# A four-layer graph network in fp32: other column halves and order in its expert layers, additions between weight units, and a new order in its attention

## Chip, cores and metric

One Trainium2 (trn2) chip, one core. The metric is the device time of one execution in microseconds (us), lower is better. TensorE is PE below, VectorE is DVE, ScalarE is ACT, GpSimd is POOL, SyncE is SP.

## What is computed

Four layers, each a graph part and a feed-forward part with residuals, on 625 nodes of 768 features, all in fp32. Cut to what matters here:

```python
x = x + gnn0(layernorm(x))         # g0: softmax aggregation, then 768 -> 1536 -> 768, + bias + input
x = x + moe0(layernorm(x))         # f0: 8 experts, top 2, hidden 192, gelu
x = x + gcn(layernorm(x))          # g1: two graph convolutions
x = x + moe1(layernorm(x))         # f1: 8 experts, top 2, hidden 128, silu, balanced by importance
x = x + gat(layernorm(x))          # g2: attention, 8 heads x 128, relu, then 1 head x 768
x = x + soft_slots(layernorm(x))   # f2
x = x + rgcn3(layernorm(x))        # g3: three relational layers
x = x + moe3(layernorm(x))         # f3: 8 experts, top 2, hidden 192, gelu

# one expert layer (f0, f1, f3)
logits = x @ gate.T;  probs = softmax(logits);  w, i = top_k(probs, 2)
# f1 alone: importance = probs.sum(axis=0); running = 1 + 0.1 * (importance - 1) + 0.01; w = w / running[i]
combine[t, i] = w / sum(w)
y = sum_e combine[:, e] * (act(x @ w1[e]) @ w2[e])

# the attention
e = leaky_relu(a_src[src] + a_dst[dst], 0.2)
alpha = exp(e - max over the node's edges);  out = sum(alpha * h[src]) / sum(alpha)
```

## The kernel before

The 625 nodes are five tiles of 125 (padded to 626 columns where nodes are columns). Every dense fp32 product is three fp32r matmuls on a high and a low part of each operand (`three`, L2501 to L2503: high by high, low by high, high by low). The weights stream in as units of 128 x 768: SP loads each into a ring of three raw slots, POOL splits it into `w_hi` (L867) and `w_lo` (L870), and PE's use of a unit frees its slot (`unit_used`). POOL works through the units in the order in which it is written; other work of POOL stands between them.

All orders are written by hand: each engine's program is a list of steps, and the steps wait on semaphores. `plan_groups` only simulates PE's groups to hand out the eight PSUM banks: a group that opens a bank waits until the bank's last user was read.

**g0.** The MLP's up part has twelve units, its down part twelve more. Between the two, POOL adds the bias to the residual of the five tiles (L881, five additions of 125 x 768), and only then splits unit 12, the down part's first.

**An expert layer** (`expert_layer`, L2640). The normalised rows are transposed tile by tile on PE (`turn_behind`, L2510); ACT copies them as `xT_hi` (L938) and DVE makes `xT_lo` (L1488). The transposes of the last tile are left over and done inside the layer. `router(c)` multiplies the nodes of half c with the gates (L2656, L2658): half 0 is columns 0 to 311 (`CH`), so it waits for the low parts of tiles 0 to 2, half 1 for all. `up(s, j)` is a job: one unit of 128 hidden features against one half of the columns, 18 matmuls. Job j is unit j // 2, half j % 2. `router(1)` stands behind job 0, its transposes for DVE (L2674) behind job 1, f1's sum over all probabilities (L2681) behind job 3. DVE works out the routing (`route`, L1694 to L1744) meanwhile; behind job 5 (`EXPERT_LAG` 6) PE waits for the result `combine`, transposes it (L2688) and, from then on, broadcasts a row of it for each job (L2698), by which DVE weighs the job's activation in one of six slots `tmp`.

```python
router(0)
turn_behind(s)(NT - 1)
for j, spread in enumerate(spread_after(jobs)):
    if j < jobs: up(s, j)
    if j == 0: router(1)
```

**The attention** (g2). PE makes h1 in 20 groups of 125 x 256 (matmuls of 256 columns); ACT copies each out (L1213) and has other steps between the copies. Among these are `powers(h, s)` for the heads h = 0 and 1 and the source tiles s = 0 to 4: two exponentials (L1204, L1205) with which DVE makes `greater_branch` (L2061). Two buffers of them may wait for DVE at most, so the fourth waits for DVE's first. `weights_of_edges` (L2067) is DVE's loop over s; beside it run the ten maxima of scores of later heads (`greatest_score`, L2009). Then, head by head, PE multiplies h1 with the weights (`head_product`, L2919), DVE takes the totals (`head_total`, L2127) and makes the next head's scores (L2086), ACT the means (`head_mean`, L1262) and exponentials. The second part of the attention starts with its own product g2b (five groups for each half), whose banks are fixed numbers 0 to 4.

## Time and profile before

| | |
|---|---|
| median of 3 runs | 1725.19 us (1724.49 to 1728.24) |
| the profiled execution | 1721.06 us, of which the traced span is 1719.3 us |
| PE busy | 1670.1 us (97% of the span), 10227 matmuls |
| DVE, ACT, POOL busy | 53%, 26%, 41% |
| granted clock of PE | nine tenths of full or more in 39 of 40 slices, eight tenths in the second |

Read it so: PE is busy nearly always, so what the profile shows as PE's idle time in front of an instruction, with its releaser, is where time can go or come from. A row of a timeline gives the start, the duration, the engine, line and operation, output <- input, shapes, how many like instructions it joins, and in brackets the idle time before it and what ended that.

### The profile page before, as it was taken

To read this page: it belongs to the slowest core of one execution; us is meant where nothing else is said; L and a number is where in the kernel's file an instruction comes from. 1 tells how busy PE (TensorE), PEld (TensorE's weight loads), DVE (VectorE), ACT (ScalarE), POOL (GpSimd) and SP (SyncE) were. 2 spreads that over 40 slices of the span, in tenths; PEclk is the share of its full clock that TensorE was granted. 3 is DMA by queue.
4 is the path that set the end of the run, shared out by engine and by line. 5 is a ranking of instruction groups with operands and counts; after the bars stand their busy time and mean duration, and the time that the engine had idled before them with its cause. 6 is when DMAs were issued, how large, how long until landed. Compare 5 with 4: busy or idle time off the path is not lost.

```text
span 1719.3 us, 25796 instructions
## 1 busy us (share of the span) xinstructions
PE 1670.1 (97%) x10227; PEld 1571.7 (91%) x10227; DVE 919.6 (53%) x1860; ACT 452.6 (26%) x867; POOL 697.7 (41%) x432
## 2 busy tenths in 40 slices
PE   8799999999999998899999999999999999999999
PEld 7699999997999998899477889899999999998999
DVE  8993537417776688878588453513112141235731
ACT  7443113303223147834132311101001111112310
POOL 1026855661544631350020375442643434342663
PEclk9899999999999999999999999999999999999999
DMA  2002222323212210014010122110211112110222
GB/s 91 1 28 65 76 65 65 132 91 138 65 47 58 78 50 19 12 37 143 19 33 1 31 77 64 54 48 28 83 58 53 58 44 59 52 56 30 65 74 73
DMA packets 41999, 99.83 MB, mean 58 GB/s; under 512 B 10508, under 2 KB 12142, under 8 KB 41894
## 3 DMA queue, kind: packets, MB, share of 16 engines
q1 hardware_dynamic: 37828, 87.87, 16.8%
q10 hardware_dynamic: 4066, 10.46, 1.7%
q8 instruction: 79, 1.29, 0.3%
q14 instruction: 26, 0.21, 0.0%
HBM read 96.39 MB, written 1.92 MB: 57 GB/s over the span
## 4 chain that ended last, share of the span: by engine, by line
PE 84%; DVE 11%; ACT 2%; issue 1%; POOL 1%; POOLq 0%; DVEq 0%; ACTq 0%
PE bank L2501 10%; PE bank L2502 10%; PE bank L2503 10%; PE banks L2501 9%; PE banks L2503 9%; PE banks L2502 9%; PE banks L2995 3%; PE bank L2995 3%; PE banks L3170 2%; PE banks L3175 2%; PE bank L3170 2%; PE bank L3175 2%; PE bank L2919 2%; DVE src_hot L1557 1%; DVE tmp L1893 1%
## 5 line engine op out<-in xcount | busy, mean ns | idle before, releaser
L867 POOL TENSOR_TENSOR w_hi<-raw,ones_r 128x768 fp32r<-128x768 f32 (+1 forms) x192 | 295.8, 1541 | 911.8 <-PE bank L2503 334.1
L870 POOL TENSOR_TENSOR w_lo<-raw,w_hi 128x768 fp32r<-128x768 f32 (+1 forms) x192 | 370.5, 1930 | 15.1
L2501 PE MATMUL bank<-w_hi,xT_hi 128*125 128x384 f32 (+2 forms) x564 | 188.6, 334 | 1.9 <-DVE small L2034 1.5
L2503 PE MATMUL bank<-w_hi,xT_lo 128*125 128x384 f32 (+2 forms) x564 | 187.5, 333 | 0.0
L2502 PE MATMUL bank<-w_lo,xT_hi 128*125 128x384 f32 (+2 forms) x564 | 187.5, 332 | 0.0
L2501 PE MATMUL banks<-w_hi,xT_hi 128*125 128x384 f32 (+2 forms) x436 | 151.0, 346 | 0.0
L2503 PE MATMUL banks<-w_hi,xT_lo 128*125 128x384 f32 (+2 forms) x436 | 150.5, 345 | 0.0
L2502 PE MATMUL banks<-w_lo,xT_hi 128*125 128x384 f32 (+2 forms) x436 | 150.3, 345 | 0.0
L1684 DVE TENSOR_TENSOR hT_lo<-tmp,hT_hi 128x312 fp32r<-128x312 f32 (+1 forms) x88 | 94.2, 1077 | 42.0 <-ACT hT_hi L1012 41.6
L2501 PEld LDWEIGHTS bank<-w_hi,xT_hi 128*125 128x125 f32 x564 | 104.6, 186 | 5.1 <-DVE small L2034 1.7
L2502 PEld LDWEIGHTS bank<-w_lo,xT_hi 128*125 128x125 f32 x564 | 104.6, 186 | 2.3
L2503 PEld LDWEIGHTS bank<-w_hi,xT_lo 128*125 128x125 f32 x564 | 104.5, 185 | 2.4
L2396 DVE TENSOR_TENSOR through_lo<-banks,through_hi 125x384 fp32r<-125x384 f32 (+1 forms) x45 | 25.5, 578 | 138.1 <-ACT through_hi L1417 138.1
L2501 PE MATMUL bank<-w_hi,hT_hi 128*125 128x384 f32 x276 | 93.5, 339 | 1.3 <-ACT mean L1262 0.9
L2503 PE MATMUL bank<-w_hi,hT_lo 128*125 128x384 f32 x276 | 93.2, 338 | 0.0
L2502 PE MATMUL bank<-w_lo,hT_hi 128*125 128x384 f32 x276 | 93.1, 337 | 0.0
L2501 PE MATMUL banks<-xT_hi,w_hi 128*128 128x312 f32 (+1 forms) x282 | 87.5, 310 | 0.1
L2502 PE MATMUL banks<-xT_lo,w_hi 128*128 128x312 f32 (+1 forms) x282 | 86.8, 308 | 0.0
L2503 PE MATMUL banks<-xT_hi,w_lo 128*128 128x312 f32 (+1 forms) x282 | 86.6, 307 | 0.0
L2396 DVE TENSOR_TENSOR through_lo<-bank,through_hi 125x384 fp32r<-125x384 f32 (+1 forms) x45 | 25.7, 582 | 110.6 <-ACT through_hi L1417 110.6
L2501 PE MATMUL banks<-w_hi,hT_hi 128*125 128x384 f32 x244 | 82.7, 339 | 1.6 <-POOL w_lo L870 1.6
L2501 PEld LDWEIGHTS banks<-w_hi,xT_hi 128*125 128x125 f32 x436 | 80.9, 186 | 2.9 <-DVE xT_lo L1635 0.3
(592 smaller groups left out, 3909.7 us busy)
## 6 DMA issues: line engine op xcount, KB each, us to landing
raw<-wa SPq DMA_DIRECT2D x92, 384.0 KB, 3.1
raw<-wc SPq DMA_DIRECT2D x76, 384.0 KB, 3.1
raw<-wb SPq DMA_DIRECT2D x28, 448.0 KB, 3.3
w_rows<-w_in ACTq DMA_DIRECT2D x1, 3072.0 KB, 12.8
bias<-bias_in ACTq DMA_DIRECT2D x6, 384.0 KB
w_first<-w_in ACTq DMA_DIRECT2D x1, 2304.0 KB, 9.7
w_down<-w_down_in SPq DMA_DIRECT2D x8, 288.0 KB, 5.3
w_up<-w_up_in SPq DMA_DIRECT2D x1, 2304.0 KB, 10.8
```

The costliest lines, as they stand in the source:

```text
L867: pool.tensor_tensor(w_hi[:, k, 0:width], raw[:, k, 0:width], ones[:, 0:1].to_broadcast([P, width]), ALU.mult).then_inc(S("unit_high"), 1)
L870: pool.tensor_tensor(w_lo[:, k, 0:width], raw[:, k, 0:width], f(w_hi[:, k, 0:width]), ALU.subtract).then_inc(S("unit_split"), 1)
L1557: TS(src_hot[0:TN, k], iota[:, 0:NODES], source[:, t:t + 1], None, ALU.is_equal).then_inc(S(label + "_hot"), 1)
L1684: TT(hT_lo[:, m, c0:c0 + cn], tmp[:, i % TSLOTS, 0:cn], f(hT_hi[:, m, c0:c0 + cn]), ALU.subtract).then_inc(S(s + "_low"), 1)
L2396: TT(through_lo[c][:, n, 0:width], bank(key + "_through", i)[0:TN, 0:width], f(through_hi[c][:, n, 2 - 2 * c:2 - 2 * c + width]), ALU.subt ...
L2501: tell_used(pe.matmul(dst, l_hi, r_hi, start=start, stop=False))
L2502: pe.matmul(dst, l_hi, r_lo, start=False, stop=False)
L2503: return pe.matmul(dst, l_lo, r_hi, start=False, stop=stop)
L2919: last = pe.matmul(dst[0:TN, at:at + HEAD_DIM + 1], prob_of("g2p", h)[:, s, n * TN:(n + 1) * TN], h1[:, s, h, 0:HEAD_DIM + 1], start=s == ...
L2995: ins = pe.matmul(bank("R", d)[0:TN, c * cn:(c + 1) * cn], source[:, s * TN:(s + 1) * TN], target[:, at], start=t == r_first(p, r) and wid ...
L3170: tell_used(pe.matmul(dst[0:TN, 0:counted + cw], rel[:, r, s, at], through_hi[c][:, s, begin:begin + counted + cw], start=s == 0, stop=False))
L3175: last = pe.matmul(dst[0:TN, counted:counted + cw], rel[:, r, s, at], through_lo[c][:, s, 0:cw], start=False, stop=s == NT - 1)
```

## The change

1. The expert layers split the nodes into columns 0 to 249 and 250 to 625 (`EXPERT_CH`). `router(0)` waits for two tiles. The first four jobs are units 0 and 1 with half 0, then units 0 and 1 with half 1. The left transposes stand behind job 0, `router(1)` behind job 1, its transposes behind job 2, f1's sum behind job 5, and the routing is awaited behind job 6. There are seven slots for activations, each 376 wide.
2. POOL waits for the routing (`combine`) before it splits unit 4 of each expert layer (`held_units`).
3. In g0 POOL does one residual addition and then one unit, five times.
4. In the attention's `weights_of_edges`, two of the maxima go ahead of each `greater_branch`, where they stood behind it; ACT does the head-1 powers of s = 3 and 4 behind the last copy of h1, where they stood between the copies.
5. g2b's groups open banks 4, 5, 0, 1, 2, where they opened 0, 1, 2, 3, 4.

```diff
+EXPERT_CH = [(0, 2 * TN), (2 * TN, NP - 2 * TN)]
-EXPERT_LAG = 6
-IMPORTANCE = 3
+EXPERT_LAG = 7
+IMPORTANCE = 5
+ROUTED_UNIT = 4
+EXPERT_SLOTS = 7
+ROUTER_JOB = 1
+POWERS_BESIDE = 3
+LAST_BANKS = (4, 5, 0, 1, 2)
...
     if s == "g0" and j < 6:
         return j % 3, j // 3
+    if s != "g0" and j < 4:
+        return j % 2, j // 2
     return j // 2, j % 2
...
+        def held_units(engine, first, count, body):
+
+            last = first + count
+            for s in ("f0", "f1", "f3"):
+                hold = FIRST_UNIT["u", s] + ROUTED_UNIT
+                if first < hold < last:
+                    ring_units(engine, first, hold - first, body)
+                    engine.wait_ge(*E(s + "_combine", 4))
+                    first = hold
+            ring_units(engine, first, last - first, body)
...
             for n in range(NT):
                 pool.wait_ge(*E("g0_doubled", n + 1))
                 pool.tensor_tensor(x[0:TN, n], x[0:TN, n], bias[0:TN, 0:D], ALU.add).then_inc(S("g0_residual"), 1)
+                u = UP_UNITS["g0"] + n
+                split(UNIT)(u, u // RING, u % RING)
...
-                if i > NEXT_SHIFT:
+                if NEXT_SHIFT < i <= NEXT_SHIFT + POWERS_BESIDE:
                     powers("g2p", 1, i - NEXT_SHIFT - 1)
...
+            for s in range(POWERS_BESIDE, NT):
+                powers("g2p", 1, s)
             lesser_shifts(2)
...
                 for s in range(NT):
+                    for other, d in beside[2 * s:2 * s + 2]:
+                        if d == 0:
+                            await_group(dve, "g2p_asB", 2 * other + 1)
+                        greatest_score("g2p", other, d)
                     greater_branch("g2p", h, s)
...
-                    for other, d in beside[2 * s:2 * s + 2]:
-                        if d == 0:
-                            await_group(dve, "g2p_asB", 2 * other + 1)
-                        greatest_score("g2p", other, d)
...
-                    pe.wait_ge(*E(s + "_xT_low", (6, 2 * NT)[c]))
+                    pe.wait_ge(*E(s + "_xT_low", (4, 2 * NT)[c]))
...
                 router(0)
-                turn_behind(s)(NT - 1)
...
                     if j == 0:
+                        turn_behind(s)(NT - 1)
+                    if j == ROUTER_JOB:
                         router(1)
-                    if j == 1:
+                    if j == ROUTER_JOB + 1:
                         pe.wait_ge(*E(s + "_routerT_read", 2))
```

The same change as the order of instructions, at three places. POOL in g0, between the last up unit and the down units, before; L881 is the residual addition, L867 and L870 split a unit (high, low):

```order
L870 TENSOR_TENSOR w_lo<-raw,w_hi 128x768
L782 REGISTER_ALU
L782 COMPARE_AND_BRANCH
L881 TENSOR_TENSOR x<-x,bias 125x768 x5
L782 UNCONDITIONAL_BRANCH
L782 ISA
L866 ISA
L867 TENSOR_TENSOR w_hi<-raw,ones_r 128x768
L869 REGISTER_ALU
L870 TENSOR_TENSOR w_lo<-raw,w_hi 128x768
```

and changed (the addition is L918 there, the split L904 and L907):

```order
L918 TENSOR_TENSOR x<-x,bias 125x768
L904 TENSOR_TENSOR w_hi<-raw,ones_r 128x768
L907 TENSOR_TENSOR w_lo<-raw,w_hi 128x768
L918 TENSOR_TENSOR x<-x,bias 125x768
L904 TENSOR_TENSOR w_hi<-raw,ones_r 128x768
L907 TENSOR_TENSOR w_lo<-raw,w_hi 128x768
```

Unit 12 stands behind one addition where it stood behind five.

DVE at the start of the attention's weights of head 0, before; L2009 is a maximum of scores (with the read of its result), L2061 the greater branch of one source tile, L2071 the product with the adjacency:

```order
L2061 SCALAR_TENSOR_TENSOR prob_early_77<-prob_early_77,lesser 125x626
L2009 ISA edge_scores_141,small<-banks,maskT 125x628
L2009 ISA small 125x1
L2009 ISA edge_scores_142,small<-banks,maskT 125x628
L2009 ISA small 125x1
L2061 SCALAR_TENSOR_TENSOR prob_early_77<-prob_early_77,lesser 125x626
L2071 SCALAR_TENSOR_TENSOR prob_early_77<-prob_early_77,adj 125x1252
```

and changed (L2051, L2103 and L2117 are the same three operations):

```order
L2051 ISA edge_scores_148,small<-banks,maskT 125x628
L2051 ISA small 125x1
L2051 ISA edge_scores_149,small<-banks,maskT 125x628
L2051 ISA small 125x1
L2103 SCALAR_TENSOR_TENSOR prob_early_83<-prob_early_83,lesser 125x626
L2051 ISA edge_scores_148,small<-banks,maskT 125x628
L2051 ISA small 125x1
L2051 ISA edge_scores_149,small<-banks,maskT 125x628
L2051 ISA small 125x1
L2103 SCALAR_TENSOR_TENSOR prob_early_83<-prob_early_83,lesser 125x626
L2117 SCALAR_TENSOR_TENSOR prob_early_83<-prob_early_83,adj 125x1252
```

Two more maxima come ahead of the first greater branch; five branches and ten maxima are left in all.

ACT at the end of the copies of h1, before; L1213 is a copy, L1204 and L1205 the two exponentials of one source tile:

```order
L1213 ACTIVATE h_68<-bank 125x2x128 [waits group_closed]
L1204 ACTIVATE prob_early_78<-uB_early_80,small 125x626 [waits greater]
L1205 ACTIVATE lesser<-uB_early_80,small 125x626
L1213 ACTIVATE h_68<-bank 125x2x128 [waits group_closed]
L1204 ACTIVATE prob_early_78<-uB_early_80,small 125x626 [waits greater]
L1205 ACTIVATE lesser<-uB_early_80,small 125x626
L1246 ACTIVATE uB_75<-banks 125x626 [waits group_closed]
```

and changed (the copy is L1253, the exponentials L1244 and L1245):

```order
L1253 ACTIVATE h_68<-bank 125x2x128 [waits group_closed] x2
L1244 ACTIVATE prob_early_84<-uB_early_86,small 125x626 [waits greater]
L1245 ACTIVATE lesser<-uB_early_86,small 125x626
L1244 ACTIVATE prob_early_84<-uB_early_86,small 125x626 [waits greater]
L1245 ACTIVATE lesser<-uB_early_86,small 125x626
L1286 ACTIVATE uB_81<-banks 125x626 [waits group_closed]
```

The last two copies no longer stand behind exponentials that wait for DVE.

## Rows read from the trace of the kernel before

**Rows 1.** The page: span and busy time of the engines.

```profile
span 1719.3 us, 25796 instructions
PE 1670.1 (97%) x10227; PEld 1571.7 (91%) x10227; DVE 919.6 (53%) x1860; ACT 452.6 (26%) x867; POOL 697.7 (41%) x432
```

**Rows 2.** Waits of PE: engine, line, what for; total us, times, longest.

```profile
PE bank L2919 <- ACT mean L1262: 7.3, 7, 1.6
...
PE banks L2656 <- issue: 0.7, 1, 0.7
```

**Rows 3.** Timeline of POOL and PE where g0's up part ends.

```profile
176.76 10.04 POOL L881 TENSOR_TENSOR x<-x,bias 125x768 f32<-125x768 f32 x5
186.76 1.47 POOL L867 TENSOR_TENSOR w_hi<-raw,ones_r 128x768 fp32r<-128x768 f32 x1
188.31 1.93 POOL L870 TENSOR_TENSOR w_lo<-raw,w_hi 128x768 fp32r<-128x768 f32 x1
...
190.30 0.44 PE L2501 MATMUL banks<-w_hi,hT_hi 128*125 128x384 f32 x1 [1.60 <-POOL w_lo L870]
```

**Rows 4.** Timeline of PE, unbroken streams of 312, 384 and 256 columns: first and last.

```profile
178.07 0.30 PE L2501 MATMUL bank<-xT_hi,w_hi 128*128 128x312 f32 x1
...
180.69 0.31 PE L2501 MATMUL bank<-xT_hi,w_hi 128*128 128x314 f32 x1
...
250.33 0.34 PE L2503 MATMUL banks<-w_hi,hT_lo 128*125 128x384 f32 x1
...
252.10 0.80 PE L2510 MATMUL bank<-ident,xn_f 125*128 125x125 f32 x6
...
631.70 0.28 PE L2501 MATMUL bank<-w_hi,xT_hi 128*125 128x256 f32 x1
...
632.76 0.46 PE L2825 MATMUL banks<-rows_K,sel 128*125 128x314 f32 x2
```

**Rows 5.** Timeline of PE, DVE and ACT where f0 and f3 start.

```profile
258.35 0.31 PE L2656 MATMUL bank<-xT_hi,gates 128*16 128x312 f32 x1 [0.85 <-DVE xT_lo L1488]
...
1579.66 0.30 PE L2656 MATMUL bank<-xT_hi,gates 128*16 128x312 f32 x1 [2.73 <-issue]
...
1579.86 1.03 ACT L956 ACTIVATE xn<-x,small 125x768 f32<-125x768 f32 x1 [0.83 <-DVE small L1481]
...
1581.37 0.80 PE L2510 MATMUL banks<-ident,xn 125*128 125x125 f32 x6
...
1582.62 1.00 DVE L1488 TENSOR_TENSOR xT_lo<-banks,xT_hi 128x500 fp32r<-128x500 f32 x2 [0.23 <-ACT xT_hi L938]
```

**Rows 6.** Timeline of DVE in f1's routing.

```profile
530.22 0.17 DVE L1724 TENSOR_SCALAR small<-banks 125x8 f32<-125x8 f32 x1 [1.19 <-PE banks L2681]
...
530.87 1.11 DVE L1729 TENSOR_TENSOR small<-small 125x40 f32<-125x40 f32 x1
...
532.46 1.43 DVE L1734 TENSOR_TENSOR small<-small 125x40 f32<-125x40 f32 x1
...
534.64 0.18 DVE L1744 COPY cpad<-hot_hi 125x40 f32<-125x40 f32 x1
```

**Rows 7.** Timeline of DVE, ACT and PE in the attention, heads 0 and 1.

```profile
648.64 0.81 DVE L2061 SCALAR_TENSOR_TENSOR prob_early<-prob_early,lesser 125x626 f32<-125x626 f32 x1 [2.60 <-ACT lesser L1205]
649.37 0.81 DVE L2009 CUSTOM_DVE_ANT_0 edge_scores<-banks,maskT 125x628 f32<-125x628 f32 x1
...
666.82 0.82 ACT L1204 ACTIVATE prob_early<-uB_early,small 125x626 f32<-125x626 f32 x1 [2.13 <-DVE prob_early L2061]
...
668.66 5.76 PE L2919 MATMUL bank<-h,prob_early 125*125 125x129 f32 x50 [2.26 <-ACT h L1213]
...
674.46 0.16 DVE L2127 TENSOR_SCALAR small<-bank 125x2 f32<-125x2 f32 x1 [1.07 <-PE bank L2919]
```

**Rows 8.** Windows, one head: stretch, us, busy (x) of PE, PEld, DVE, ACT, POOL.

```profile
683.26:690.93 7.67, 6.94 (x60) 6.64 (x59) 7.64 (x10) 7.07 (x14) 0.16 (x1) 1.00 0.00 0
```

**Rows 9.** Timeline of PE, the start of g2b.

```profile
730.25 0.41 PE L2501 MATMUL bank<-w_hi,hT_hi 128*125 128x384 f32 x1 [0.95 <-ACT mean L1262]
```

More of the change, by code:

```diff
@@ L162, in job_of, with columns_of @@
         return j % 3, j // 3
+    if s != "g0" and j < 4:
+        return j % 2, j // 2
     return j // 2, j % 2
+def columns_of(s, c):
+    return (CH if s == "g0" else EXPERT_CH)[c]
 LEFT_TURNS = {"f0": 1, "f1": 1, "f3": 1, "g2": TURN_LAG}
@@ L355, in plan_groups @@
         for n in range(NT):
-            add("g2b", c * NT + n, "g2_h2", c * NT + n + 1, held=True, b=n)
+            add("g2b", c * NT + n, "g2_h2", c * NT + n + 1, held=True, b=LAST_BANKS[n])
         ends = closing[opened:]
@@ L574, in network @@
         maskT = at_("maskT", [TN, NT, 2 * HALF_ROWS], bf16, mask_off)
+        last_slots = {s: [at_(f"{s}_slot{i}", [P, EXPERT_CH[1][1]], f32, off)
+                          for i, off in enumerate((XT + up32(KD * NP * 4), HT + 8 * NP * 4 if s == "f1" else NM + 20480))]
+                      for s in ("f0", "f1", "f3")}
         gat_small = mask_off + up32(NT * 2 * HALF_ROWS * 2)
@@ L617, in network @@
         tmp = at_("tmp", [P, TSLOTS, WIDE], f32, tmp_off)
+        expert_tmp = at_("expert_tmp", [P, TSLOTS - 1, EXPERT_CH[1][1]], f32, tmp_off)
+        assert (TSLOTS - 1) * EXPERT_CH[1][1] <= TSLOTS * WIDE
         iota = new("iota", [TN, NP], i16)
@@ L767, in col, with slot_of @@
             return cols[:, a:b] if i is None else cols[:, a + i:a + i + 1]
+        def slot_of(s, j, cn):
+            if s == "g0":
+                return tmp[:, j % TSLOTS, 0:cn]
+            k = j % EXPERT_SLOTS
+            return expert_tmp[:, k, 0:cn] if k < TSLOTS - 1 else last_slots[s][k - TSLOTS + 1][:, 0:cn]
         def await_group(engine, label, i):
@@ L884, in _ @@
             after = shared + n_shared
-            ring_units(pool, UP_UNITS["g0"], shared - UP_UNITS["g0"], split(UNIT))
+            held_units(pool, UP_UNITS["g0"] + NT, shared - UP_UNITS["g0"] - NT, split(UNIT))
             for i, u in enumerate(range(shared, after)):
@@ L916, in _ @@
             ring_units(pool, UNITS_A, UNITS_B, split(UNIT_WIDE, n_shared))
-            ring_units(pool, UNITS_A + UNITS_B, UNITS_C, split(UNIT, n_shared))
+            held_units(pool, UNITS_A + UNITS_B, UNITS_C, split(UNIT, n_shared))
         @block.scalar
@@ L1009, in high @@
                     m, c = job_of(s, i)
-                    c0, cn = CH[c]
+                    c0, cn = columns_of(s, c)
                     act.wait_ge(*E(full, i + 1))
-                    act.activation(hT_hi[:, m, c0:c0 + cn], tmp[:, i % TSLOTS, 0:cn], ACT.Copy
+                    act.activation(hT_hi[:, m, c0:c0 + cn], slot_of(s, i, cn), ACT.Copy
                                    ).then_inc(S(s + "_high"), 1)
@@ L1018, in hidden @@
                         m, c = job_of(s, j)
-                        cn = CH[c][1]
-                        if made <= j - TSLOTS:
+                        cn = columns_of(s, c)[1]
+                        if made <= j - slots:
                             high(made)
@@ L1023, in hidden @@
                         await_group(act, s + "_hidden", j)
-                        if j >= TSLOTS:
-                            act.wait_ge(*E(s + "_low", j - TSLOTS + 1))
-                        act.activation(tmp[:, j % TSLOTS, 0:cn], bank(s + "_hidden", j)[:, 0:cn], func,
+                        if j >= slots:
+                            act.wait_ge(*E(s + "_low", j - slots + 1))
+                        act.activation(slot_of(s, j, cn), bank(s + "_hidden", j)[:, 0:cn], func,
                                        **scale_bias(m)).then_inc(S(s + "_activated"), 1)
@@ L1034, in expert_layer @@
                 normal_rows(s)
-                for c, (c0, cn) in enumerate(CH):
+                for c, (c0, cn) in enumerate(EXPERT_CH):
                     await_group(act, s + "_routerT", c)
@@ L1673, in hidden_low @@
                     if j < jobs and weigh:
-                        cn = CH[j % 2][1]
+                        cn = columns_of(s, job_of(s, j)[1])[1]
                         dve.wait_ge(*E(s + "_activated", j + 1))
                         await_group(dve, s + "_cB", j)
-                        TT(tmp[:, j % TSLOTS, 0:cn], tmp[:, j % TSLOTS, 0:cn], bank(s + "_cB", j)[:, 0:cn], ALU.mult
+                        TT(slot_of(s, j, cn), slot_of(s, j, cn), bank(s + "_cB", j)[:, 0:cn], ALU.mult
                            ).then_inc(S(s + "_weighted"), 1)
@@ L2529, in up @@
                 m, c = job_of(s, j)
-                c0, cn = CH[c]
+                c0, cn = columns_of(s, c)
                 u = FIRST_UNIT["u", s] + m
@@ L2707, in seed @@
                                   start=True, stop=False)
-                down(s + "d", s + "_down", hT_hi, hT_lo, lambda k: pe.wait_ge(*E(s + "_low", 2 * k + 2)), seed=seed,
+                down(s + "d", s + "_down", hT_hi, hT_lo, lambda k: pe.wait_ge(*E(s + "_low", max(2 * k + 2, 4))), seed=seed,
                      turn=turn_behind("g2") if s == "f1" else None, left=LEFT_TURNS["g2"])
```

15 lines of the change are left out of this document (9 added, 6 removed).

## The prediction

> **What bounds the kernel now.** I read the page first. PE is busy 1670.1 of 1719.3 us and no other engine comes near that [rows 1]. So a change pays only if it takes idle time away in front of a PE instruction, or makes PE's stream itself shorter. Next I read the waits of PE for those at the changed places [rows 2], and then the timeline around each, to see what the releaser did and what would be late next. The idle time in brackets counts from the modelled end of the matmul before. In an unbroken stream matmuls are 0.31 us long and start 0.146 us apart [rows 4], so each overlaps the next by about 0.16 us, and a wait costs PE that much more than the bracket says. I count 0.15 us more for each, as the loss from start to start.
>
> **g0's additions.** POOL does five in 10.04 us and only then splits unit 12, in 1.47 + 1.93 us; PE stands 1.60 us for that [rows 3], 1.75 with the overlap. Afterwards unit 12 waits for one addition, 2.0 us: it is split at 176.76 + 2.0 + 3.4 = 182.2, while PE is free at 188.7. The other four additions now stand before units 13 to 16. POOL needs 2.0 + 3.4 = 5.4 us for such a pair. PE needs 30 matmuls of 384 columns for each unit of the down part, 30 x 0.177 = 5.3 us [rows 4]. Unit 13's pair would be done at 187.6 and is wanted at 194; over the next three units the lead shrinks by 0.1 us each. The last addition ends later than before by three to four splits, about 14 us, near 201; its reader is the down part's output, which comes after most of 12 units x 5.3 us. So the whole 1.75 us goes: **-1.7**.
>
> **Start of the expert layers.** In f0 PE waits 0.85 us for tile 2's low part, in f3 2.73, in f1 0.7 [rows 5, 2]. Now router(0) needs two tiles alone, whose low parts come one tile (some 3 us) earlier, so these waits go, with the overlap 1.0, 2.9 and 0.85 us. What is late next is the left tile 4. Its normalised rows come from ACT at 1579.86 + 1.03 = 1580.89 in f3 [rows 5]. Router(0) starts near 1576.8 there, takes 12 x 0.115 = 1.4, job 0 takes 18 x 0.115 = 2.1, so PE is at the transposes at 1580.3 and waits 0.6. In f0 and f1 these rows are ready in time, by the same sum. Router(1) then stands behind the transposes (0.6) and job 1 (2.1), 2.7 us from their start. The low part is done 1582.62 + 1.00 - 1581.37 = 2.25 us after it [rows 5]. That leaves 0.4 us, the thinnest margin of this change. f0 **-1.0**, f3 -2.9 + 0.7 = **-2.2**.
>
> **f1's sum of probabilities** moves from behind job 3 to behind job 5, and the routing is awaited behind job 6. So one short job, 2.1 us, covers DVE's chain from the sum to `combine`, where two jobs of 2.6 each did. The chain ran from 530.22 to 534.64 + 0.18, 4.6 us, of which two operations on 125x40 took 1.11 and 1.43 where others of that shape took 0.18 [rows 6]. Both lie beside a split on POOL. The hold before unit 4 takes that split away, so I take the two at 0.2 each: 4.6 - 2.15 = 2.45, with 0.35 us for the two handovers 2.8, against 2.1. A new wait of 0.7 us. Below: none, if the chain is shorter still; above: 2.8, if the contention stays. f1 in all -0.85 + 0.7, **-0.2**.
>
> **The hold on POOL.** Unit 4 is split after `combine`: 3.4 us, of which the transposes of `combine` (0.6), a broadcast or two (0.3) and job 7 (376 columns, 18 x 0.173 = 3.1) cover 4.0. In f0 and f3 there is no PE wait on the routing before, so a faster chain gives nothing. I cost it at nothing; uncovered, it would cost at most 0.5 us per layer.
>
> **The attention.** DVE idles 2.60 us before the first greater branch, with maxima to do that stand behind it. ACT in turn waits 2.13 us for DVE at 666.82, and the copy of h1 behind that holds PE's first head product 2.26 us [rows 7], 2.4 with the overlap. Two parts of the change meet here. ACT's powers 3 and 4 go behind the last copy, so the copy follows its bank directly and PE starts at 668.66 - 2.4 = 666.2. And two maxima fill the gap on DVE: 2 x 0.73 = 1.46 us (0.73 from start to start in rows 7), so DVE is ready for its totals at 674.46 - 1.07 - 1.46 = 671.9, where PE's product now ends at 674.4 - 2.4 = 672.0. From there DVE is the bound: a head takes 7.67 us, of which DVE is busy 7.64 [rows 8], PE waits 7.3 us in all for the means [rows 2], and so a shift at the start of the heads lasts to their end. **-2.4**, with 1.07 if only PE had moved and 1.46 if only DVE had: the second alone would give nothing, as PE's product would hold DVE.
>
> **g2b's banks.** PE waits 0.95 us for the means that still lie in bank 0 [rows 9], 1.1 with the overlap. Bank 4 is free sooner, and two groups of three matmuls, 6 x 0.177 = 1.06 us, pass before bank 0 is wanted: **-1.1**, or 0 if bank 4's or 5's own last reader is as late.
>
> **The split of the columns.** (12 + 8 + 12) x 18 = 576 pairs of matmuls are 250 and 376 wide, where they were 312 and 314. The streams read (180.69 - 178.07) / 18 = 0.1456 us for 312 columns, (252.10 - 250.33) / 10 = 0.177 for 384, (632.76 - 631.70) / 9 = 0.1178 for 256 [rows 4]. By columns from the nearest row, 250 takes 115.0 ns and 376 takes 173.3: 288.3 for the pair against 291.2, 2.9 ns x 576 = 1.7 us. The streams of 256 and 384 are short, so I take **-1.3**, between 0 and -1.7. The upper bound is that a 250-wide matmul is paced by what is the same in all of them, its weight load of 128 columns, and keeps the 312's 0.1456: the pair is then 145.6 + 173.3 = 318.9 ns, +27.7 x 576 = +16.0. The 256-wide stream at 0.1178, with loads of 128x125, speaks against that.
>
> Here a rule speaks against this part. The Trainium skill, "TensorE: Matmul & The Clock Gate", section "Back-to-back issue gap", gives N / 2.4 + 2.5 ns for N columns on the full clock, and section "LDWEIGHTS (loading the stationary operand)" 107 ns for a load of 128 columns as a floor beside it. By it the pair takes 107 + 159 = 266 ns, and took 133 + 133 = 266: the split would be worth 0 and the sum below 1.3 us smaller. The rows are above it by 10% at each width, 145.6 against 132.5 for 312, so I go by the rows.
>
> **The sum**: 1.7 + 1.0 + 0.2 + 2.2 + 2.4 + 1.1 + 1.3 = 9.9 us. The profiled execution took 1721.06, the median of three runs is 1725.19, 4.1 above it. The sum is of one profiled execution, 1711.2 after; on the footing of the median **1715.3 us**. No time under about 0.2% (3.4 us) can be told from no change here.
>
> **The rivals.**
> - *The pair costs what it did*: all but the split happens, 1715.3 + 1.3 = 1716.6. For it: the rows' gain of 1% rests on short streams. Against: three widths agree on ns per column to 1.5%, in the order 312, 384, 256. The skill's page named above would have this.
> - *Waits come back behind the ones removed*: router(1) late in each layer (up to 0.6 us x 3 if the low part is 1 us late, as DVE's operations at times are), f1's chain at its long price (+2.1), DVE still late for the first totals (+1.0). Two or three of these: 1715.3 + 3 to 6 = 1718 to 1721. For it: the margins are 0.4 us. Against: each needs its own cause.
> - *The removed waits were cover for others*: the time DVE or POOL used up while PE stood is missed right after, in f3 and the attention above all, and PE loses there what it gained, 4 to 7 us with the case above. 1722 to 1728, no difference that can be told. Against: the engines released at those places idle for over 1 us soon after.
> - *The short matmul is bound by its weight load*, the slower side: 250 columns at the 312's pace, 1715.3 + 1.3 + 16.0 = about 1733. It decides from 1725.19 + 3.4 on, which is 13.3 us / 576 = 23 ns, a pitch of 138 ns where I expect 115. Against it stands the stream of 256 columns; for it, only that those weights were used in another order and place.
> - *More*: the second splits and additions free DVE elsewhere, 2 to 4 us below, 1711 to 1713.
>
> **How the numbers follow.** Forecast 1715.3 with its own bounds (1713.5 to 1717): 0.55. The pair unchanged: 0.12. Waits come back: 0.14. Cover lost: 0.08. Weight load: 0.05. More: 0.06. Faster by over 0.2% (below 1721.7) takes the first three and the last, 0.87; within 0.2% 0.08; slower 0.05. The range holds the forecast, the unchanged pair, most of the returning waits and most of the last case: 1710.5 to 1720.5. The remainder, about 0.2, lies above for the greater part. The runs before spread from 1724.49 to 1728.24, which moves the whole by a us or two and is in the range.
>
> **What would show each step.** Right: unit 12's low part lands by 183 and no wait of PE for it; the first down unit begins within 0.2 us of the last up job; no wait ahead of router(0) in f0, f1 and f3, and 0.6 us ahead of f3's left transposes; about 0.7 us of PE's waiting for `combine` in f1; the first head product starts without a wait for a copy of h1, and DVE's totals 2.4 us sooner; g2b without a wait for the means; job starts 18 x 0.115 = 2.07 and 18 x 0.173 = 3.1 us apart. Wrong: 250-wide matmuls over 0.125 us apart (then the split costs), a wait before router(1) in all three layers, a PE wait for unit 4, or heads longer than 7.7 us, since then the shift in the attention is eaten up. A median above 1721 would say that the sum's large terms, f3 and the attention, were not there.

## The result, and the profile after

The changed kernel takes 1713.20 us (median of 4, 1712.50 to 1714.41) against 1724.84 us (median of 4, 1723.35 to 1728.24) before. The ratio is 0.9935, with an interval of 0.9922 to 0.9947: 0.65% faster, and that is clear of the 0.2%. I had forecast 1715.3 and a gain of 9.9 us; the medians differ by 11.6. The two profiled executions differ by less, 7.8 us (1721.06 and 1713.25), and the experiments tell why.

The page after, span and busy time, against [rows 1]:

```profile
span 1711.5 us, 25768 instructions
...
PE 1670.7 (98%) x10227; PEld 1572.0 (92%) x10227; DVE 920.4 (54%) x1860; ACT 451.3 (26%) x867; POOL 698.9 (41%) x432
```

PE has as many matmuls and as much busy time as before; the 7.8 us are idle time that went. The waits of PE after (engine, line, what for; total, times, longest), against [rows 2]. The changed file's lines are about 40 further down: L2963 is the head product, L2552 the transposes of normalised rows, L2731 those of `combine`.

```profile
PE bank L2963 <- ACT mean L1302: 7.3, 7, 1.5
...
PE bank L2552 <- ACT xn L995: 1.1, 2, 0.5
...
PE bank L2731 <- DVE cpad L1786: 0.4, 1, 0.4
```

The 7.3 us for the means are unchanged. The waits for unit 12, for router(0), for the copy of h1 and for bank 0 are no longer there. Two small new ones are: 0.5 us for the rows of the left tile in f3 (the other of the two was there before), and 0.4 for the routing in f1. At each place, with the answers to [rows 3, 5, 6, 7]; first POOL and PE in g0:

```profile
177.40 2.08 POOL L918 TENSOR_TENSOR x<-x,bias 125x768 f32<-125x768 f32 x1
179.44 1.47 POOL L904 TENSOR_TENSOR w_hi<-raw,ones_r 128x768 fp32r<-128x768 f32 x1
180.99 1.97 POOL L907 TENSOR_TENSOR w_lo<-raw,w_hi 128x768 fp32r<-128x768 f32 x1
...
189.17 0.34 PE L2543 MATMUL banks<-w_hi,hT_hi 128*125 128x384 f32 x1
```

Unit 12 is split at 182.96, and PE comes to it 6.2 us later without a stop. The start of f3:

```profile
1571.23 0.35 PE L2698 MATMUL banks<-xT_hi,gates 128*16 128x250 f32 x1
...
1575.47 0.65 PE L2552 MATMUL bank<-ident,xn 125*128 125x125 f32 x4 [0.53 <-ACT xn L995]
...
1577.43 0.41 DVE L1530 TENSOR_TENSOR xT_lo<-banks,xT_hi 128x250 fp32r<-128x250 f32 x1
...
1578.27 0.34 PE L2698 MATMUL bank<-xT_hi,gates 128*16 128x376 f32 x1
```

Router(0) follows the transposes directly. The left transposes wait 0.53 us for ACT, and router(1) comes 0.43 us after the last low part (1577.43 + 0.41), so the thin margin held. f1's routing:

```profile
531.83 0.17 DVE L1766 TENSOR_SCALAR small<-banks 125x8 f32<-125x8 f32 x1 [4.13 <-PE banks L2724]
...
532.47 0.20 DVE L1771 TENSOR_TENSOR small<-small 125x40 f32<-125x40 f32 x1
...
533.15 0.20 DVE L1776 TENSOR_TENSOR small<-small 125x40 f32<-125x40 f32 x1
...
534.34 0.65 PE L2731 MATMUL bank<-ident,cpad 125*128 125x125 f32 x4 [0.42 <-DVE cpad L1786]
```

The two operations that took 1.11 and 1.43 us [rows 6] take 0.20 each. The chain is 2.45 us, and PE waits 0.42. The attention:

```profile
645.53 0.81 DVE L2103 SCALAR_TENSOR_TENSOR prob_early<-prob_early,lesser 125x626 f32<-125x626 f32 x1 [1.14 <-ACT lesser L1245]
...
662.23 0.38 ACT L1253 ACTIVATE h<-bank 125x256 f32<-125x256 f32 x1 [0.67 <-PE bank L2545]
...
663.11 5.66 PE L2963 MATMUL bank<-h,prob_early 125*125 125x129 f32 x50
...
668.52 0.45 DVE L2169 TENSOR_SCALAR small<-bank 125x3 f32<-125x3 f32 x2
```

DVE idles 1.14 us where it idled 2.60, the copy follows its bank, and PE's head product starts without a wait.

From the starts of PE's instructions in the two profiles each place has a price of its own (us, before and after):

| stretch of PE's work | before | after | gain | forecast |
|---|---|---|---|---|
| g0, first up matmul to first down matmul | 64.97 | 63.21 | 1.76 | 1.7 |
| f0, last matmul before its last transposes to its down part | 75.37 | 74.08 | 1.3 | 1.0, and 0.5 of the split |
| f1, the same | 54.21 | 53.66 | 0.55 | 0.2, and 0.3 |
| attention, first h1 matmul to the last head product | 119.92 | 117.35 | 2.6 | 2.4 |
| from there to g2b's first | 1.75 | 0.56 | 1.2 | 1.1 |
| f3, as f0 | 75.94 | 73.59 | 2.35 | 2.2, and 0.5 |

The gains sum to 9.7 us. The span fell by 7.8, since two stretches in which nothing was changed came out longer: 0.6 us before g0's first up matmul and 1.2 us between the start of f2 and the end of g3.

### The profile page after: what moved, and what is told of

Same layout as the page of the kernel before. It is cut to its first block, busy times and chain, and to the rows that moved or that the text cites. A ratio compares the mean times of both kernels' runs of the same rounds, so it can differ in the third digit from the quotient of the medians.

```text
span 1711.5 us, 25768 instructions
## 1 busy us (share of the span) xinstructions
PE 1670.7 (98%) x10227; PEld 1572.0 (92%) x10227; DVE 920.4 (54%) x1860; ACT 451.3 (26%) x867; POOL 698.9 (41%) x432
## 4 chain that ended last, share of the span: by engine, by line
PE 85%; DVE 11%; ACT 2%; issue 1%; POOL 0%; DVEq 0%; POOLq 0%; ACTq 0%
PE bank L2543 10%; PE bank L2545 10%; PE bank L2544 10%; PE banks L2543 9%; PE banks L2545 9%; PE banks L2544 9%; PE bank L3039 3%; PE banks L3039 3%; PE bank L3214 3%; PE bank L3219 3%; PE banks L3214 2%; PE banks L3219 2%; PE bank L2963 2%; DVE src_hot L1599 1%; DVE tmp L1935 1%; PE banks L2644 1%
## 5 line engine op out<-in xcount | busy, mean ns | idle before, releaser
L904 POOL TENSOR_TENSOR w_hi<-raw,ones_r 128x768 fp32r<-128x768 f32 (+1 forms) x192 | 298.0, 1552 | 905.4 <-PE banks L2545 311.3
L907 POOL TENSOR_TENSOR w_lo<-raw,w_hi 128x768 fp32r<-128x768 f32 (+1 forms) x192 | 369.6, 1925 | 15.1
L2543 PE MATMUL banks<-w_hi,hT_hi 128*125 128x384 f32 x260 | 88.4, 340 | 0.4 <-DVE h_lo L2229 0.4
L2545 PE MATMUL bank<-w_hi,hT_lo 128*125 128x384 f32 x260 | 87.9, 338 | 0.0
L2543 PE MATMUL bank<-w_hi,hT_hi 128*125 128x384 f32 x260 | 87.9, 338 | 0.0
L1459 ACT ACTIVATE through_hi<-bank 125x384 fp32r<-125x384 f32 (+1 forms) x45 | 22.9, 509 | 246.3 <-PE bank L2545 195.7
L2545 PE MATMUL banks<-w_hi,hT_lo 128*125 128x384 f32 x260 | 87.8, 338 | 0.0
L2544 PE MATMUL bank<-w_lo,hT_hi 128*125 128x384 f32 x260 | 87.7, 337 | 0.0
L2544 PE MATMUL banks<-w_lo,hT_hi 128*125 128x384 f32 x260 | 87.7, 337 | 0.0
L2543 PE MATMUL banks<-xT_hi,w_hi 128*128 128x376 f32 (+3 forms) x264 | 83.0, 314 | 0.1
L2545 PE MATMUL banks<-xT_hi,w_lo 128*128 128x376 f32 (+3 forms) x264 | 82.4, 312 | 0.0
L2544 PE MATMUL banks<-xT_lo,w_hi 128*128 128x376 f32 (+3 forms) x264 | 82.3, 312 | 0.0
```

The costliest lines, as they stand in the source:

```text
L904: pool.tensor_tensor(w_hi[:, k, 0:width], raw[:, k, 0:width], ones[:, 0:1].to_broadcast([P, width]), ALU.mult).then_inc(S("unit_high"), 1)
L907: pool.tensor_tensor(w_lo[:, k, 0:width], raw[:, k, 0:width], f(w_hi[:, k, 0:width]), ALU.subtract).then_inc(S("unit_split"), 1)
L1459: act.activation(through_hi[c][:, n, 2 - 2 * c:2 - 2 * c + width], bank(key + "_through", i)[0:TN, 0:width], ACT.Copy).then_inc(S(key + "_ ...
L2543: tell_used(pe.matmul(dst, l_hi, r_hi, start=start, stop=False))
L2544: pe.matmul(dst, l_hi, r_lo, start=False, stop=False)
L2545: return pe.matmul(dst, l_lo, r_hi, start=False, stop=stop)
```

## Experiments

Each was run beside the kernel before on the same chip: `r_before`, `r_holdalone`, `r_sum6` and `r_banks` on one (before 1724.32), the others on another (before 1723.75 to 1723.89). All but three undo or move something in the changed kernel. Differences in the runs are against `r_change` (median 1713.14); for `r_sum6` and `r_banks` they hold the 0.4 to 0.6 us between the two chips as well. Intervals of the ratios are 0.13% wide to each side, so one part's 1 or 2 us can't be told in the runs; where it matters I read the stretch of the profile.

### The change again

No edit.

> The changed kernel once more, unaltered, beside the kernel before on the same chip. Theory (a sum of single waits, each gone or halved): -9 to -10 us against before in the profiled spans, as the profiled pair of executions differed by 7.8 us (1713.25 against 1721.06) while the medians differed by 11.6 (1713.20 against 1724.84), so the runs' difference should come out between, 8 to 12 us. Rival (something in the changed kernel gains beyond the places that the profile shows): the runs differ by 12 us or more again and the profiled spans by 11 or more too.

1713.14 us against 1723.75 (ratio 0.9936, 0.9923 to 0.9950): 10.6 us, span 1711.4. The times are within 2 us of each other (1712.13 to 1714.04), and those of before within 3.7. The span against the first profile of before is again 7.9 us shorter. So the runs gain 3 us more than the pair of profiles, twice. The 10.6 us of the runs is in the theory's 8 to 12, but neither theory had the profiles right: the spans didn't come up to 9 or 10, and didn't come up to 11.

### The attention, both parts and each alone

```diff
-POWERS_BESIDE = 3
+POWERS_BESIDE = 5            # r_powers, and with the next in r_attention
...
                 for s in range(NT):
-                    for other, d in beside[2 * s:2 * s + 2]: ...
                     greater_branch("g2p", h, s)
...
+                    for other, d in beside[2 * s:2 * s + 2]: ...   # r_maxima
```

> The changed kernel with both parts of the attention undone (maxima behind the greater branch, head 1's last powers between the copies). Theory: PE waits 2.3 us for the last copy of h1 again, and from the first head product to g2b everything is 2.4 us later than in the changed kernel; the whole is +2.4 us. Rival (heads are paced by ACT or DVE with slack that absorbs a late start): the first head product is 2.4 us later but the start of g2b by under 1 us, the whole +1 or less.

> The changed kernel with only the order of ACT's head-1 powers undone. Theory (the two parts share one chain, DVE to ACT's powers to the copy to PE): the maxima that fill DVE's gap bring DVE's branches of head 1 forward by 1.5 us, so ACT waits about 0.7 us for DVE where it waited 2.1, PE's first head product is 0.8 to 1.0 us later than in the changed kernel, g2b too, the whole +0.9. Rival (the powers' order alone does it): PE waits 2.3 us again and the whole is +2.4.

> The changed kernel with only DVE's order undone (maxima behind the greater branch). Theory: PE's first head product starts as early as in the changed kernel, but DVE comes to its totals of head 0 1.5 us later, so the heads behind, paced by DVE, and g2b are 1.3 to 1.5 us later, the whole +1.4. DVE idles 2.6 us before its first branch again. Rival (the maxima only fill time that nobody needs): no place behind moves by over 0.3 us, the whole +0.3 or less.

In the runs: both undone 1715.96 (+2.8), powers 1713.92 (+0.8), maxima 1713.79 (+0.7). In the profiles, from h1's first matmul to g2b's: +2.50, +0.88 and +0.66 us over the changed kernel. With the powers undone ACT waits little, and the copy holds PE little; ACT and PE of that kernel:

```profile
663.27 0.82 ACT L1244 ACTIVATE prob_early<-uB_early,small 125x626 f32<-125x626 f32 x1 [0.55 <-DVE prob_early L2103]
...
665.12 1.15 PE L2963 MATMUL bank<-h,prob_early 125*125 125x129 f32 x8 [0.69 <-ACT h L1253]
```

The wait of 2.13 us [rows 7] became 0.55, and that of 2.26 became 0.69: the 1.46 us of maxima take effect through ACT too. The two parts are worth 2.5 together; undone alone each costs under 1, so they share the same chain. That theory held. Read the other way round, the maxima alone keep 2.50 - 0.88 = 1.6 us and the powers alone 2.50 - 0.66 = 1.8: each gives most of the whole without the other. In the third kernel DVE comes to its totals at 670.32, 1.5 us later than in the changed kernel with 0.3 taken off for its later h1:

```profile
670.32 0.22 DVE L2169 TENSOR_SCALAR small<-bank 125x3 f32<-125x3 f32 x2
```

but g2b starts only 0.66 later, where I expected 1.3 to 1.5. About 0.8 us of lateness on DVE is absorbed before the first later head; the theory had the place right and the price twice too high.

### The residual additions

```diff
-                u = UP_UNITS["g0"] + n
-                split(UNIT)(u, u // RING, u % RING)
...
-            held_units(pool, UP_UNITS["g0"] + NT, shared - UP_UNITS["g0"] - NT, split(UNIT))
+            held_units(pool, UP_UNITS["g0"], shared - UP_UNITS["g0"], split(UNIT))
```

> The changed kernel with the five residual additions in one block again, before the split of unit 12. Theory: PE waits 1.6 us for unit 12's low part, f0 starts 1.7 us later than in the changed kernel, the whole +1.7. Rival (the wait was made up later by a lead that POOL or DVE then lacks): the wait comes back, and f0's first router is later by under 1 us.

```profile
191.26 0.44 PE L2541 MATMUL banks<-w_hi,hT_hi 128*125 128x384 f32 x1 [1.63 <-POOL w_lo L907]
```

The wait is back, the stretch up to it is 64.99 us again (before 64.97, changed 63.21), and all of the 1.8 us is still there where f0's down part starts. In the runs it is 1713.68 (+0.5), too little for them to show. Four of its five executions have a mean clock of 0.995 where four of the changed kernel's five have 0.994, and 0.001 is 1.7 us: by that its usual execution has one stretch less at half clock, which hides the 1.8 (its profile has one in f2, the changed kernel's has two). The price is read from the profile.

### The banks of g2b

```diff
-LAST_BANKS = (4, 5, 0, 1, 2)
+LAST_BANKS = (0, 1, 2, 3, 4)
```

> The changed kernel with g2b's groups on banks 0 to 4 again. Theory: PE waits 0.95 us for the means in bank 0, 1.1 from start to start, the whole +1.1. Rival (the wait only moves to the user of another bank): g2b starts 1.1 later but its sixth group at the same time, the whole within 0.2.

1714.82 (+1.7, on the other chip).

```profile
726.14 0.41 PE L2543 MATMUL bank<-w_hi,hT_hi 128*125 128x384 f32 x1 [0.95 <-ACT mean L1302]
```

PE waits 0.95 us for the means, and g2b is 1.17 us later against the head product; at f2's start 1.0 of it remains. The wait goes where the banks are moved, and does not come back behind.

### The column split and the early router

```diff
-EXPERT_CH = [(0, 2 * TN), (2 * TN, NP - 2 * TN)]
+EXPERT_CH = CH
...
-                    pe.wait_ge(*E(s + "_xT_low", (4, 2 * NT)[c]))
+                    pe.wait_ge(*E(s + "_xT_low", (6, 2 * NT)[c]))
```

> The changed kernel with halves of 312 and 314 columns in the expert layers, router 0 therefore waiting for three tiles, everything else as changed. Theory: the waits before router 0 come back, 0.85, 0.7 and 2.7 us, and the wait for the left tile's rows in f3 (0.5) goes, net +3.9 us with the overlaps; the matmuls' pitch sum is 290.4 to 291.4 ns a pair, so the split itself is worth 0.5 us, the whole about +4.5. Rival (the pair is worth what I predicted, 1.3 us, or more): +5.2 or more. Rival (the early router matters little, since the waits move behind it): under +2.

1717.16 (+4.0; ratio to before 0.9958, 0.9944 to 0.9971), beside an expected +4.5. The three waits are back. But f3 alone, from its transposes to its down part, is 3.9 us longer than in the changed kernel, and the wait does not account for it. PE at its router(0), and then windows (us, busy and instructions of PE, PEld, DVE, ACT, POOL, granted clock, DMA share, GB/s):

```profile
1574.23 0.30 PE L2698 MATMUL banks<-xT_hi,gates 128*16 128x312 f32 x1 [2.72 <-issue]
...
1575.00:1579.00 4.00, 4.00 (x19) 3.59 (x18) 1.00 (x2) 1.20 (x3) 0.00 (x0) 0.57 0.30 102
1579.00:1583.00 4.00, 4.00 (x31) 4.00 (x30) 1.58 (x3) 1.14 (x3) 0.00 (x0) 1.00 0.00 0
```

Behind the wait PE runs on its lower level, 1.2 GHz, for most of 4 us (mean 0.57): 19 matmuls where the next 4 us have 31. That costs 4 x (1 - 0.57) = 1.7 us. The split itself is the smallest part. In f0 of the changed kernel a stream of 250 columns:

```profile
294.17 0.28 PE L2543 MATMUL banks<-xT_hi,w_hi 128*128 128x250 f32 x1
...
296.27 0.27 PE L2742 MATMUL banks<-cT,select 128*128 128x250 f32 x1
...
296.38 0.33 PE L2543 MATMUL bank<-xT_hi,w_hi 128*128 128x376 f32 x1
...
299.48 0.33 PE L2742 MATMUL bank<-cT,select 128*128 128x376 f32 x1
```

is (296.27 - 294.17) / 18 = 116.7 ns apart, one of 376 (299.48 - 296.38) / 18 = 172.2. Over the jobs of the three layers, from a job's start to the next instruction, the means are 117.2 and 173.3, and for 312 and 314 columns in the kernel before 146.5 and 145.2: 290.5 against 291.7 a pair, 1.2 ns x 576 = 0.7 us (0.9 against this experiment's own halves). A line through 117.2 and 173.3 leaves about 6 ns at no columns; a part like that doesn't go away with the split.

The three stretches are 1.3, 0.7 and 3.9 us longer than in the changed kernel, 5.9 in all, and the runs show 4.0. The profile has six stretches at half clock like the changed kernel's: one more in f3, one fewer in f2. So the +4.0 came near the expected +4.5 partly by luck, since the fall of the clock in f3 was not in the theory and one elsewhere was missing.

### The hold on POOL

```diff
                     ring_units(engine, first, hold - first, body)
-                    engine.wait_ge(*E(s + "_combine", 4))
                     first = hold
```

> The changed kernel without POOL's hold before unit 4 of each expert layer. Theory: POOL's splits lie beside DVE's routing again; its small 125x40 operations that meet a split take 1.1 to 1.9 us where they take 0.2. In f1 the wait of PE for the routing grows from 0.4 us by 0.9 to 2.2 us; in f0 and f3 the routing has slack of about 1.5 to 2 us in the changed kernel, so at most a few tenths there. The whole +1 to +2. Rival (contention is not what stretches them, or the hold costs elsewhere): the operations stay at 0.2 us, the whole within 0.4 us.

1723.24 us (1720.21 to 1726.91), 10.1 us slower than the changed kernel and level with the kernel before (0.9994, 0.9985 to 1.0003). That is the largest effect of any part, where I had expected 1 to 2. In f0 the routing ends at 281.77 where it ends at 275.56 in the changed kernel (0.7 of that is a later start). DVE and POOL, and PE behind them:

```profile
277.68 1.47 POOL L903 TENSOR_TENSOR w_hi<-raw,ones_r 128x768 fp32r<-128x768 f32 x1 [1.48 <-PE bank L2542]
277.86 1.33 DVE L1775 TENSOR_TENSOR small<-small 125x40 f32<-125x40 f32 x1
279.22 1.80 POOL L906 TENSOR_TENSOR w_lo<-raw,w_hi 128x768 fp32r<-128x768 f32 x1
279.23 1.83 DVE L1777 CAST hot_hi<-small 125x40 fp32r<-125x40 f32 x1
...
281.83 0.43 PE L2730 MATMUL bank<-ident,cpad 125*128 125x125 f32 x2 [2.31 <-DVE cpad L1785]
```

Here four of the 125x40 operations beside POOL's splits take 1.3 to 1.8 us; in the changed kernel they take 0.2:

```profile
274.43 0.20 DVE L1776 TENSOR_TENSOR small<-small 125x40 f32<-125x40 f32 x1
274.66 0.18 DVE L1778 CAST hot_hi<-small 125x40 fp32r<-125x40 f32 x1
```

Each long one ends with the split beside it: 277.86 + 1.33 = 279.19 behind 277.68 + 1.47 = 279.15, and 279.23 + 1.83 = 281.06 behind 279.22 + 1.80 = 281.02. All 18 operations on 125x40 that take over 0.6 us in the three layers of this kernel end 0.04 to 0.06 us after an operation of POOL. Those on 125x8 in the midst of a split (MAX8, FIND_INDEX8) take their usual 0.15 us. So the long ones don't run slowly, they wait for POOL's operation to end. The Trainium skill, "SBUF — State Buffer", section "SBUF: two separate sides", describes the port pair that DVE and GpSimd share as an exclusive lock that is held for the whole instruction, so that the other one waits. The rows agree, with the 0.04 to 0.06 us above. PE waits 2.3, 2.5 and 2.2 us in the three layers, and behind each wait the clock falls; windows behind that of f0:

```profile
282.00:284.00 2.00, 2.00 (x12) 2.00 (x12) 1.96 (x8) 0.00 (x0) 0.00 (x0) 0.71 0.60 197
284.00:286.00 2.00, 2.00 (x8) 2.00 (x7) 0.84 (x1) 0.00 (x0) 0.00 (x0) 0.50 0.04 8
286.00:288.00 2.00, 2.00 (x16) 2.00 (x15) 0.55 (x2) 0.10 (x1) 0.34 (x1) 0.94 0.00 0
```

0.58 + 1.00 + 0.12 = 1.7 us lost, once in each layer of this execution. The stretches of f0, f1 and f3 are 4.1, 3.7 and 4.0 us longer than in the changed kernel. Of these 11.7 us, 5.1 are the clock. The profiled execution is the slowest of the eleven (1726.91 at 0.989, eleven stretches at half clock). The median one, at 0.992, has about eight, two more than the changed kernel's six: an estimate of 6.6 + 2 x 1.7 = 10.0 us, beside the 10.1 of the runs. By this the waits of PE come each time, and not all three falls behind them do. The rival "within 0.4 us" is out, and so is my size.

### The hold alone

```diff
 # in the kernel before: held_units as in the change, with ROUTED_UNIT = 4
-            ring_units(pool, UP_UNITS["g0"], shared - UP_UNITS["g0"], split(UNIT))
+            held_units(pool, UP_UNITS["g0"], shared - UP_UNITS["g0"], split(UNIT))
...
-            ring_units(pool, UNITS_A + UNITS_B, UNITS_C, split(UNIT, n_shared))
+            held_units(pool, UNITS_A + UNITS_B, UNITS_C, split(UNIT, n_shared))
```

> The kernel before with POOL's hold before unit 4 of each expert layer alone. Theory (the hold is worth much only behind the new order, which leaves the routing less cover): the 125x40 operations that took 1.1 to 1.9 us come down to 0.2, combine is 2 to 4 us earlier in f0 and f3 and 2 in f1, PE waited for it in none of them, and the whole is within 1 us of before, up to 2 us if it spares a stretch at half clock. Rival (the hold itself is most of the gain of the change): 5 us or more faster.

1723.87 us against 1724.32, ratio 1.0001 (0.9992 to 1.0010): nothing. Yet in f0 the routing ends at 275.50 where it ended at 278.22. The hold is worth nothing in the old order, where PE did not wait for the routing, and 10 us in the new one.

### What two equal kernels differ by

The kernel before, no edit.

> The kernel before, unaltered, once more, for its profile and for what two equal kernels differ by. Runs show its span 1.7 us longer for each 0.001 less of mean granted clock, and most of its executions at 0.993 where the profiled one was at 0.995. Theory: in this profile one or two stretches at half clock of 3.4 us each (1.7 us lost each) stand where the first profile has none, and the likeliest places are right behind PE's two longest changed waits, 2.3 us in the attention and 2.7 us at f3's start. Rival: the extra stretches lie elsewhere (g0's aggregation, f2), where nothing was changed. The time itself: ratio 1.000 within 0.001.

1724.06 against 1724.32, ratio 0.9999 (0.9990 to 1.0009). The profile came out as the first (1718.9, clock 0.995), so it could not show where the usual execution loses more. The list of executions shows how much: those of before at 0.995 took 1720.7 to 1722.3 us, those at 0.993 mostly 1723 to 1725, those at 0.991 1727.1 to 1728.1. That is about 3 us for 0.002. Both profiles of before are of the less frequent kind. The hold-alone kernel, equal to it in time, was profiled at 0.993. It has the 2.7 us wait at f3's start too:

```profile
1580.19 0.30 PE L2668 MATMUL bank<-xT_hi,gates 128*16 128x312 f32 x1 [2.71 <-issue]
...
1581.00:1585.00 4.00, 4.00 (x21) 3.47 (x20) 1.92 (x4) 2.30 (x6) 0.00 (x0) 0.57 0.34 102
```

and loses 1.7 us right behind it, which neither profile of before does (their clock is 1.00 there). Its other extra stretch is in f2, where nothing was changed, and where the changed kernel has two too:

```profile
838.00:842.00 4.00, 4.00 (x8) 1.12 (x7) 0.00 (x0) 0.00 (x0) 0.00 (x0) 0.57 0.01 2
852.00:856.00 4.00, 4.00 (x17) 2.77 (x18) 1.77 (x4) 0.00 (x0) 0.00 (x0) 0.57 0.01 4
```

The second is also in the first profile of before, the first is not. So both halves of the expectation came true in part: one stretch behind a changed wait, one elsewhere.

### f1's sum, one job earlier and one later

```diff
-IMPORTANCE = 5
+IMPORTANCE = 4            # r_sum4;  6 in r_sum6
```

> The changed kernel with f1's sum over the probabilities behind job 4 instead of job 5. Theory: DVE's first part of the routing ends at 527.7 in f1, about when job 4 ends, so the chain from the sum is covered by jobs 5 and 6, and the wait for the routing (0.42 us, 0.58 from start to start) goes: -0.6 us in the profile, not to be told from zero in the runs. Rival: the wait only moves to the sum itself, within 0.1 us.

> The changed kernel with f1's sum behind job 6, directly ahead of the wait for the routing: a longer wait of PE with no contention in it. Theory: the chain from the sum to combine (2.5 us) is covered by nothing, PE waits about 2.5 us in f1 where it waited 0.42, and the clock falls to half for 3.4 us right behind it as it did behind the waits of 2.3 to 2.7 us of the kernel without the hold, 1.7 us more: +2.3 + 1.7 = +4 against the changed kernel. Rival (only a wait together with other load brings the clock down, as the first profile of before has 2.7 us in f3 and keeps the clock): +2.3 alone.

Earlier: 1711.92 us (1710.62 to 1712.40, ratio to before 0.9926, 0.9913 to 0.9940), the fastest of all kernels here, 1.2 below the change. In the profile the wait for the routing is gone and f1 is 0.48 us shorter. The rest of the 1.2 is not told from chance. Later: 1714.44 (+1.3), but 1717.57 in the profiled execution. There:

```profile
537.32 0.65 PE L2731 MATMUL bank<-ident,cpad 125*128 125x125 f32 x4 [2.62 <-DVE cpad L1786]
...
538.00:540.00 2.00, 2.00 (x10) 2.00 (x9) 0.75 (x4) 0.00 (x0) 1.92 (x2) 0.69 0.00 0
540.00:542.00 2.00, 2.00 (x8) 2.00 (x8) 0.00 (x0) 0.00 (x0) 2.00 (x2) 0.50 0.17 18
```

a wait of 2.62 us, with no split on POOL during it, and the lower clock behind: f1 is 3.65 us longer, of which 2.2 are the wait. The executions lie at 1712.0, 1713.5, 1714.4, 1716.3 and 1717.6, over 5.5 us, where the changed kernel's lie within 2. Their mean clocks are, in this order, 0.995, 0.995, 0.994, 0.993 and 0.993, which is five, five, six, seven and seven stretches at half clock. With 1.7 us taken off for each, this kernel lies about 2.1 us above the changed one on average (an estimate; the rounding of the clock leaves nearly 1 us for each execution). So the wait seems to cost its length each time, and the fall of the clock to come with it only sometimes; only one of these executions has a profile.

## Why the prediction was right, and where it was not

**The terms.** Of the six places each is within 0.5 us of its forecast. g0's additions (1.7 forecast, 1.76 measured), the attention (2.4, 2.6) and g2b's banks (1.1, 1.2) came out as priced, and undoing each brought its wait back. How the attention's two parts combine was wrong, though their sum was right: the prediction had the maxima alone "give nothing", and they keep 1.6 us; it had the powers alone at 1.07, and they keep 1.8. The step that failed took the maxima to act only on DVE's totals. They also bring DVE's branches forward, for which ACT waits, and with ACT the copy of h1 and PE (ACT's wait of 2.13 us became 0.55).

**Start of the expert layers.** The three waits went. The new wait in f3 was put at 0.6 and is 0.53; the margin at router(1) was put at 0.4 and is 0.43. f1's new wait was put at 0.7 and is 0.42: the chain was right (2.45 forecast, 2.45 measured), the cover was under-counted.

**The split of the columns** was mis-sized. I took 1.3 us by scaling from streams of 256 and 384 columns; it is 0.7. The step that failed is "By columns from the nearest row, 250 takes 115.0 ns": it took 117.2, nearly what 256 takes (117.8), where 376 took the 173.3 that was forecast. The pace does not shrink in proportion to the columns. The rule in the Trainium skill, "TensorE: Matmul & The Clock Gate", "Back-to-back issue gap", has a fixed part, and by an estimate from it the split was worth 0. The measured 0.7 lies halfway between that estimate and my scaling, and the rule's 107 and 159 ns (estimates too) are below the 117.2 and 173.3 of these streams. I had that rival at 0.12; its time, 1716.6, missed for other reasons.

**The hold on POOL** was costed "at nothing", with an uncovered price of 0.5 us per layer. That it costs nothing was right. But the step asked only what the hold might cost, and not what the new order would cost without it: 10.1 us. For f0 and f3 that it came out was luck: no line of the prediction asks whether the routing is ready there in the new order, and without the hold it is 2.3 and 2.2 us late. In f1 I had used its effect (the two operations at 0.2 each) and bounded the other side at 2.8 us of waiting; measured without it are 2.5 us of waiting, and 1.7 at the lower clock behind it that I did not price. For f0 and f3, "a faster chain gives nothing" is true of the old order only. The new order frees units 0 and 1 in two jobs in a row, so that without the hold POOL splits three units between 269.45 and 281.02, beside nearly the whole of f0's chain.

**The sum and the medians.** The sum of the places, 9.7, is close to the 9.9 that I forecast; the profiles differ by 7.8 and the medians by 10.6 to 11.6. Around the sum lies the number of stretches at 1.2 GHz, 1.7 us each. By windows of 1 us the first profile of before has five, the changed kernel's two have six. So the pair of profiles should show 9.7 - 1.7 = 8.0, and does with 7.8. The usual execution of before, at 0.993 (about 0.007 x 1720 = 12 us lost), has seven: 9.7 + 1.7 = 11.4, near the 10.6 to 11.6.

The runs bear this out. Taking 1.71 us off each execution for each 0.001 of its mean clock below 1 (an estimate; the clock is rounded to 0.001, which leaves nearly 1 us in one execution), the kernel before lies 9.5 to 9.9 us above the changed one on average, the kernel without the hold 6.8 (its stretches gave 11.7 - 5.1 = 6.6), the one without the attention's change 2.7 (2.5), with one block of additions 2.3 (1.8), and f1's sum one job earlier 0.6 below (0.5).

My step from 1711.2 to 1715.3, "on the footing of the median", took the 4.1 us between the two as an offset that stays. It does not: the changed kernel's profile lies on its median, 1713.25 against 1713.20. So 1711.2 for the profiled execution was 2 us too low and 1715.3 for the median 2 us too high, just outside the forecast's own bounds (1713.5 to 1717), each by about one such stretch. No profile shows the usual execution of before. The hold-alone kernel, equal to it in time, has its two extra stretches right behind the wait in f3 and in f2; whether they stand there in before too is open.

**The rivals.** Waits that come back: 0.5 and 0.4 us, both in the sum. Cover lost: none. A short matmul held by its weight load: out, at 117 ns against the 138 from which it would decide. More: the median lies at the edge of its 1711 to 1713, but the places gained 9.7 us and not 2 to 4 more.

## What to carry over

Price a reordering as a whole: a part that is worth nothing by itself (the hold) can be what makes another part (an order that frees two units at once) bearable, so also ask what the new order costs without each part. Take from a profile the stretches, not the spans: two executions of the same kernel differ by whole stretches at half clock, here 1.7 us each, as much as one removed wait is worth. A wait of PE like those here (2.2 to 2.7 us) should be priced with such a stretch as a possibility, and other shares of the same columns between two matmuls as worth next to nothing (0.7 us here).

## What the runs showed of the hardware that I had not expected

- Behind idle times of PE of 2.2 to 2.7 us the granted clock fell to half, from 2.4 to 1.2 GHz, for 3.4 us, six times: f0, f1 and f3 without the hold, f3 with equal halves, f3 with the hold alone, f1 with the late sum. It did not fall behind the 2.7 us in f3 in two profiles of before, nor behind the 2.3 us in the attention in four profiles, nor behind 2.2 us ahead of head 1 in `r_maxima`. What decides between these is open.
- The spread of the times goes with that: the kernel without the hold lay over 6.7 us in 11 executions (clock 0.989 to 0.993), the kernel before over 7.4 in 11 (0.991 to 0.995), the changed one over 1.9 in five (0.993 and 0.994).
- DVE's operations on 125x40, 0.2 us alone, took 1.1 to 1.9 us beside a split on POOL and ended 0.04 to 0.06 us after one of its operations: the wait is for the rest of an operation of POOL, however small DVE's own is. The routing's chain in f0, made of about 35 small ones, grew from 7 to 13 us when three splits lay beside it.
